# GpSimd masks two more units of softmax weights per step in the first attention layer, and TensorE two fewer

## The chip, the cores and the metric
The kernel runs on one core of a Trainium2 chip. Time is device time in microseconds (us) of one execution; the median of several runs is given. The core has TensorE (PE, matrix products; its weight loads are shown apart as PEld), VectorE (DVE), ScalarE (ACT), GpSimd (POOL) and SyncE (SP), which here only issues DMAs. Each engine works through its own instructions in order, and they wait for each other by semaphores.

## The reference
A Flamingo block of two layers on 32 sequences of 112 tokens with 256 features: cross attention to 375 context rows (16 heads of 16), then a feed-forward part, and the same again with other weights and a mixture of experts. The part that the change touches is the first layer's attention, with one mask of keys for all sequences:

```python
q = split_heads(input_q @ w_q)          # (32, 16, 112, 16)
k = split_heads(input_k @ w_k)          # (32, 16, 375, 16)
v = split_heads(input_v @ w_v)
scores = jnp.einsum('bhqd,bhkd->bhqk', q, k) / jnp.sqrt(jnp.float32(D_K))
scores = jnp.where(mask == 0, jnp.float32(NEG), scores)
attn = jax.nn.softmax(scores, axis=-1)
per_head = jnp.einsum('bhqk,bhkd->bhqd', attn, v)
...
x = x + jnp.tanh(g_xattn[0]) * _L0_xattn_ref(_layernorm(x, axis=-1), ctx_1024, ctx_1024, mask_1x1xSxS2_ik1, ...)
```

A masked key must get the weight zero. That can be done in two ways: add a large negative number to its score ahead of the exponential, or multiply the weight by zero behind it.

## The kernel before, in words
The phases follow each other: weights are prepared, attention of layer 0 (about 85 to 552 us), the first feed-forward part, attention of layer 1, the experts. `attention_phase` is used for both layers.

Attention goes by steps, written out one after the other for each engine (`run_quads`, `body`), 32 sequences and a few steps more. Step s works on several sequences at once, at different stages: the context of sequence s is split into a high and a low half-precision part, the keys of sequence s-1 are made, the values and the row maxima of sequence s-3, the weights of sequence s-4 (d in the code), the output of sequence s-5. So step 4 is the first one that masks weights, and step 35 the last; steps 32 to 35 have no context left to split.

The weights of a sequence are made transposed, with 125 keys on the partitions, in 12 units: unit i is 4 heads (i // 3) by one third of the keys (i % 3), 125 x 448 numbers. For each unit:
- TensorE makes the scores in one of three banks, two products of 224 columns (`score_unit`, L944). If the unit is not in `pool_units`, it first puts the mask there by a product of mask_add with the identity, 448 columns (L940), and the scores are added on top.
- ScalarE takes the exponential into probs (`weigh_up`, L1100).
- If the unit is in `pool_units`, GpSimd multiplies probs in place by mask_keep, 0 or 1 (`mask_unit`, L724).
- At the end of the step TensorE multiplies all 12 units in order with the values (`weigh`, L962), and waits for each unit's mask or exponential as it comes to it. There is only one probs tile: the first exponential of the next step waits until these products are done.

GpSimd's step is: the masks of the units in `pool_units`, in order, and then `low_context`, twice (L789): the low part of the context, that is the input less its high part. TensorE's `make_keys` of the next step waits for both (L850 is its first product), between the first unit and the second:

```python
for i in pool_units:
    ...
    if d.exists(B):
        mask_unit(d, i)
if s.exists(B):
    low_context(s, 0)
    low_context(s, 1)
```

TensorE's step begins with `turn_maxima` of the second half (L923), unit 0, score row 2 and the first keys; score rows (L914) are what VectorE reduces to row maxima (L1272). Twice a step VectorE writes eight maxima negated to max_parts (`shift_parts`, L1281). The keys are copied by ScalarE (`high_keys`, L1108), which then goes on with units 1 to 4. SyncE's step begins with the store of turned maxima (L643) and the load of a context (`load_context`, L649), which waits for the low parts of the sequence that used the buffer before.

In layer 1 the same table of units holds; GpSimd there has the routing to the experts as well.

Of the kernel before, what the change touches and what calls it, by code (L numbers as in the profile page):

```python
# [36 lines left out]
NOBODY = 8192  # L37

POOL_UNITS = (0, 1, 3, 4, 6, 7, 9, 10)
W_SCALE = 2.0 ** 6  # L40
MASKED = float(2 ** 30)
EPS = 1e-5
# [107 lines left out]
def setup_phase(nc, m, a):  # L150


    with ExitStack() as ctx:
# [55 lines left out]
        def _(dve):  # L209
# [35 lines left out]
            for i, ((w, n), tile) in enumerate(raw.items()):  # L245
                dve.wait_ge(high_ready, i + 1)
                dve.scalar_tensor_tensor(out=m["w" + w][n][1][:, :, :], in0=tile[:, :, :], scalar=W_SCALE,
                                         in1=m["w" + w][n][0][:, :, :], op0=ALU.mult, op1=ALU.subtract)
# [7 lines left out]
            for n in range(2):  # L256
                dve.tensor_scalar(m["wo"][n][:, :, :], m["wo"][n][:, :, :], m["gate"][:, n:n + 1], None, ALU.mult)
                scale = 1.0 if n else W_SCALE
                dve.tensor_scalar(bo[n][:, :], bo[n][:, :], m["gate"][0:S, n:n + 1], scale, ALU.mult,
# [10 lines left out]
        def _(act):  # L270
# [4 lines left out]
            for (w, n), tile in raw.items():  # L275
                act.activation(m["w" + w][n][0][:, :, :], tile[:, :, :], ACT.Copy, scale=W_SCALE).then_inc(high_ready, 1)

# [221 lines left out]
def attention_phase(nc, m, layer, x_in, x_out, context, masks, q_split, mask_in, routing):  # L499
# [3 lines left out]
    with ExitStack() as ctx:  # L503
# [82 lines left out]
        work_bank = m["bank"][7]  # L586
        HALF = UNITS // 2
        HH = H // 2
        pool_units = POOL_UNITS

        ctx_rows = context.rearrange("b (c p) k -> b p c k", p=P)
        q_rows = q_split.rearrange("e g (r p) (b t) -> e b (g r) p t", p=NP, t=S)
# [34 lines left out]
        def reduced_at(quad, name):  # L627

            return len(REDUCED) * quad + REDUCED.index(name) + 1
# [86 lines left out]
        def _(pool):  # L716
# [47 lines left out]
            def pick(quad):  # L764
                slots = slice(G * (quad % 3), G * (quad % 3) + G)
                pool.wait_ge(reduced, reduced_at(quad, "inverse"))
                pool.tensor_scalar(sent_rows[:, slots, D], chance[:, :], m["gate"][0:S, 3:4], W_SCALE ** -2,
                                   ALU.mult, ALU.mult).then_inc(combined, 1)
# [302 lines left out]
        def _(act):  # L1071
# [17 lines left out]
            def copy_values(x, e, ks):  # L1089
# [3 lines left out]
                               work_bank[0:CK, 0:D * len(ks)].rearrange("p (k h r) -> p k h r", r=DK, h=H),  # L1093
                               ACT.Copy, scale=1 / W_SCALE).then_inc(v_ready, 1)

# [7 lines left out]
            def high_keys(p, j):  # L1103

                if j == 0:
                    wait(act, k_loaded[p.two], 96 * p.use2)
                act.wait_ge(k_made, KC * p.value + j + 1)
                act.activation(k_high[p.two][:, j, 0:S2], work_bank[:, 0:S2], ACT.Copy,  # L1108
                               scale=1 / W_SCALE).then_inc(k_high_ready, 1)

# [814 lines left out]
```

## Time and profile before
| | |
|---|---|
| Time, median of 3 runs | 1663.68 us (1658.14 to 1667.85) |
| Profiled execution | 1670.54 us, span 1668.9 us |
| TensorE busy | 1486.5 us, 89% of the span |
| VectorE busy | 1067.6 us, 64% |
| GpSimd busy | 853.8 us, 51% |
| ScalarE busy | 818.5 us, 49% |
| Granted TensorE clock, mean | 0.955 of full speed |

Durations of instructions overlap: a product of 448 columns is shown with 0.35 us, and the next one starts 0.19 us after it. So a cost is read from the distance between starts, not from a duration. "Idle before" in a row is the time in which the engine stood still just before it, with the engine and instruction that ended that wait. Layer 0's attention from 200 to 500 us is 22 equal steps.

### The profile page before, as it was taken

To read this page: it belongs to the slowest core of one execution; us is meant where nothing else is said; L and a number is where in the kernel's file an instruction comes from. 1 tells how busy PE (TensorE), PEld (TensorE's weight loads), DVE (VectorE), ACT (ScalarE), POOL (GpSimd) and SP (SyncE) were. 2 spreads that over 40 slices of the span, in tenths; PEclk is the share of its full clock that TensorE was granted. 3 is DMA by queue.
4 is the path that set the end of the run, shared out by engine and by line. 5 is a ranking of instruction groups with operands and counts; after the bars stand their busy time and mean duration, and the time that the engine had idled before them with its cause. 6 is when DMAs were issued, how large, how long until landed. Compare 5 with 4: busy or idle time off the path is not lost. (4 is left out here: it accounts for less than half of the span.)

```text
span 1668.9 us, 41243 instructions
## 1 busy us (share of the span) xinstructions
PE 1486.5 (89%) x15435; PEld 1082.2 (65%) x15435; DVE 1067.6 (64%) x3580; ACT 818.5 (49%) x1907; POOL 853.8 (51%) x904
## 2 busy tenths in 40 slices
PE   0889899999999499999994789999999999529997
PEld 0457678777777266666663457777777777417776
DVE  5767677777777255555545677777777777226663
ACT  3456566666666222222221456666667666314442
POOL 0077677777777000000000177778888888723442
PEclk9999899999999699999997999999999999759999
DMA  5755544544441222222214866655566553063440
GB/s 147 197 130 147 124 102 104 101 102 102 101 93 39 61 63 63 63 71 63 62 36 117 203 125 115 116 113 110 113 128 122 121 108 57 21 187 101 155 137 19
DMA packets 214248, 172.67 MB, mean 103 GB/s; under 512 B 69930, under 2 KB 207599, under 8 KB 214056
## 3 DMA queue, kind: packets, MB, share of 16 engines
q1 hardware_dynamic: 208424, 160.34, 41.8%
q0 software_dynamic: 5632, 9.78, 1.9%
q8 instruction: 119, 1.95, 0.5%
q14 instruction: 73, 0.60, 0.1%
HBM read 95.86 MB, written 41.15 MB: 82 GB/s over the span
## 5 line engine op out<-in xcount | busy, mean ns | idle before, releaser
L1100 ACT ACTIVATE probs_a<-bank 125x448 f32<-125x448 f32 x768 | 384.7, 540 | 23.7 <-PE bank L944 15.0
L724 POOL TENSOR_TENSOR probs_a<-probs_a,mask_keep 125x448 int32<-125x448 int32 x256 | 285.5, 1138 | 108.2 <-ACT probs_a L1100 108.1
L1272 DVE CUSTOM_DVE_ANT_0 masked_scores_a<-bank,mask_add_a 112x375 bf16<-112x375 f32 x512 | 262.5, 547 | 106.0 <-PE bank L914 105.5
L724 POOL TENSOR_TENSOR probs_a<-probs_a,keep_a 125x448 int32<-125x448 int32 x256 | 286.1, 1137 | 66.4 <-ACT probs_a L1100 65.0
L1272 DVE CUSTOM_DVE_ANT_0 masked_scores_a<-bank,mask_add 112x375 bf16<-112x375 f32 x512 | 261.1, 550 | 85.5 <-PE bank L914 82.0
L914 PE MATMUL bank<-k_stack_a,q_stack_a 96*128 96x375 f16 x1024 | 292.4, 326 | 5.8 <-DVE row_max_a L1272 4.6
L944 PE MATMUL bank<-q_stack_a,k_stack_a 97*128 97x224 f16 x1536 | 254.6, 261 | 11.7 <-DMA q_stack_a<-max_t_a 10.7
L944 PEld LDWEIGHTS bank<-q_stack_a,k_stack_a 97*128 97x128 f16 x1536 | 147.0, 99 | 72.7 <-DMA q_stack_a<-max_t_a 12.3
L789 POOL TENSOR_TENSOR ctx_low_a<-ctx_in_a,ctx_high_a 128x375 f16<-128x375 f32 x128 | 113.1, 904 | 146.2 <-ACT ctx_high_a L1078 146.1
L1627 PE MATMUL bank<-h0h_f,ffn_w 128*128 128x448 f16 x512 | 180.5, 352 | 0.0
L1627 PE MATMUL bank<-h0l_f,ffn_w 128*128 128x448 f16 x512 | 180.4, 352 | 0.0
L1466 POOL DMA_DIRECT2D x_after_ffn<-y_f x8 | 5.9, 741 | 333.7 <-DVE y_f L1513 333.7
L962 PE MATMUL bank<-probs_a,values_a 125*32 125x112 f32 x6144 | 161.5, 260 | 1.9 <-POOL probs_a L724 1.9
L962 PEld LDWEIGHTS bank<-probs_a,values_a 125*32 125x32 f32 x6144 | 144.8, 110 | 22.6 <-issue 19.5
L1153 ACT ACTIVATE heads_t_a<-bank 128x448 f32<-128x448 f32 x64 | 34.8, 544 | 216.7 <-PE bank L962 216.7
L914 PEld LDWEIGHTS bank<-k_stack_a,q_stack_a 96*128 96x128 f16 x1024 | 99.5, 98 | 45.2 <-DVE row_max_a L1272 13.7
L1578 ACT ACTIVATE h1h_f<-bank 128x448 f16<-128x448 f32 x64 | 34.8, 544 | 152.9 <-PE bank L1627 152.9
L871 PE MATMUL bank<-wv_high,ctx_high_a 128*128 128x256 f16 x384 | 105.3, 274 | 1.4 <-DVE k_low_a L1315 1.4
L871 PE MATMUL bank<-wv_high,ctx_low_a 128*128 128x256 f16 x384 | 104.9, 273 | 0.0
L871 PE MATMUL bank<-wv_low,ctx_high_a 128*128 128x256 f16 x384 | 104.7, 273 | 0.0
L1506 DVE SCALAR_TENSOR_TENSOR h1l_f<-bank,h1h_f 128x448 f16<-128x448 f32 x64 | 39.8, 621 | 97.3 <-ACT h1h_f L1578 97.3
L850 PE MATMUL bank<-ctx_high_a,wk_high 128*128 128x375 f16 x256 | 84.2, 329 | 6.9 <-DVE k_low_a L1315 6.6
(215 smaller groups left out, 3193.0 us busy)
## 6 DMA issues: line engine op xcount, KB each, us to landing
k_stack_a<-k_high_a SPq DMA_DIRECT2D x256, 96.0 KB, 4.0
ctx_in_a<-in_ctx_dram SPq DMA_DIRECT2D x64, 375.0 KB, 3.6
w_in_e<-in_L_ffn_W_dram SPq DMA_DIRECT2D x16, 1024.0 KB, 8.6
k_stack_a<-k_low_a SPq DMA_DIRECT2D x128, 96.0 KB, 4.5
q_stack_a<-q_split SPq DMA_DIRECT2D x128, 84.0 KB, 3.4
q_split<-high_a SPq DMA_DIRECT2D x32, 224.0 KB, 3.7
mask_in_f<-in_mask_BxSxS_if_dram SPq DMA_DIRECT2D x8, 656.2 KB, 6.4
mask_keep<-keep_f SPq DMA_DIRECT2D x8, 656.2 KB
```

Of the source, the lines that this page charges most:

```text
L724: pool.tensor_tensor(bits, bits, cols, ALU.mult).then_inc(masked, 1)
L789: pool.tensor_tensor(ctx_low[s.four][:, cols], ctx_in[s.two][:, c, :], ctx_high[s.four][:, cols], ALU.subtract).then_inc(ctx_low_ready, 1)
L850: last = pe.matmul(work_bank[:, 0:S2], w[:, c, j * P:(j + 1) * P], part[p.four][:, c * S2:(c + 1) * S2], start=c == 0 and n == 0, stop=c = ...
L871: last = pe.matmul(work_bank[:, (k % 2) * D:(k % 2 + 1) * D], part[x.four][:, at:at + P], w[:, c, :], start=c == 0 and n == 0, stop=c == K ...
L914: pe.matmul(bank_of(x, h)[:, 0:S2], q_stack[x.four][0:STACK, at:at + P], k_stack[x.four][0:STACK, (h // 2) * WIDE:(h // 2) * WIDE + S2], s ...
L944: last = pe.matmul(bank[:, half * 2 * S:(half + 1) * 2 * S], k_stack[d.four][0:ROWS, at:at + P], q_stack[d.four][0:ROWS, (2 * t + half) * ...
L962: last = pe.matmul(head_bank[QUAD * j:QUAD * (j + 1), t * S:(t + 1) * S], values[d.two][:, k, 4 * t + j, :], probs[:, i, j * S:(j + 1) * S ...
L1100: act.activation(probs[:, i, :], score_bank[i % 3][0:CK, 0:GT], ACT.Exp, scale=DK ** -0.5).then_inc(exped, 1)
L1153: act.activation(heads_t[:, :], head_bank[:, 0:GT], ACT.Copy).then_inc(heads_ready, 1)
L1272: dve.tensor_tensor_reduce(masked_scores[:, use_of[x.value, h] % 3, :], bank_of(x, h)[0:S, 0:S2], mask_add[x.four][:, 0:S2], 1.0, -LARGEST ...
L1506: dve.scalar_tensor_tensor(out=low[:, j, :], in0=z_bank[z % 4][:, 0:GT], scalar=0.0, in1=high[:, j, :], op0=ALU.max, op1=ALU.subtract).the ...
L1627: last = pe.matmul(z_bank[z % 4][:, 0:GT], w[layer][:, c, j * P:(j + 1) * P], part[:, c, :], start=c == 0 and n == 0, stop=c == chunks - 1 ...
```

## The change
Layer 0 gets a table of its own, with units 2 and 5 in it as well. Layer 1 keeps the old one.

```diff
 POOL_UNITS = (0, 1, 3, 4, 6, 7, 9, 10)
+POOL_UNITS_0 = (0, 1, 2, 3, 4, 5, 6, 7, 9, 10)
...
-        pool_units = POOL_UNITS
+        pool_units = POOL_UNITS if layer else POOL_UNITS_0
```

All later lines of the code move down by one, so L724 of before is L725 of after.

On GpSimd, in layer 0 at the last two steps with low parts and behind them; L724 is a mask, L789 a low part. Before:

```order
L724 TENSOR_TENSOR probs_a<-probs_a,mask_keep 125x448 x8
L789 TENSOR_TENSOR ctx_low_a<-ctx_in_a,ctx_high_a 128x375 x2
L724 TENSOR_TENSOR probs_a<-probs_a,mask_keep 125x448 x8
L789 TENSOR_TENSOR ctx_low_a<-ctx_in_a,ctx_high_a 128x375 x2
L724 TENSOR_TENSOR probs_a<-probs_a,mask_keep 125x448 x32
L1381 UNCONDITIONAL_BRANCH
```

And after:

```order
L725 TENSOR_TENSOR probs_a<-probs_a,mask_keep 125x448 x10
L790 TENSOR_TENSOR ctx_low_a<-ctx_in_a,ctx_high_a 128x375 x2
L725 TENSOR_TENSOR probs_a<-probs_a,mask_keep 125x448 x10
L790 TENSOR_TENSOR ctx_low_a<-ctx_in_a,ctx_high_a 128x375 x2
L725 TENSOR_TENSOR probs_a<-probs_a,mask_keep 125x448 x40
L1382 UNCONDITIONAL_BRANCH
```

Two more masks stand ahead of each pair of low parts, and the four steps without low parts have 40 masks in place of 32.

On TensorE, in a middle step of layer 0, right behind the first keys: L914 is a score row, L944 the scores of a unit, L940 a mask added by a product. Here units 1, 2, 3 and 4 are scored. Before:

```order
L914 MATMUL bank<-k_stack_a,q_stack_a 128x375
L944 MATMUL bank<-q_stack_a,k_stack_a 128x224 x2
L914 MATMUL bank<-k_stack_a,q_stack_a 128x375
L940 MATMUL bank<-ident_b,mask_add 128x448
L944 MATMUL bank<-q_stack_a,k_stack_a 128x224 x4
L914 MATMUL bank<-k_stack_a,q_stack_a 128x375 x2
L944 MATMUL bank<-q_stack_a,k_stack_a 128x224 x2
```

And after:

```order
L915 MATMUL bank<-k_stack_a,q_stack_a 128x375
L945 MATMUL bank<-q_stack_a,k_stack_a 128x224 x2
L915 MATMUL bank<-k_stack_a,q_stack_a 128x375
L945 MATMUL bank<-q_stack_a,k_stack_a 128x224 x4
L915 MATMUL bank<-k_stack_a,q_stack_a 128x375 x2
L945 MATMUL bank<-q_stack_a,k_stack_a 128x224 x2
```

The mask's product ahead of unit 2 is gone. Later in the same step, at unit 5, ahead of the turning of the heads (L970). Before:

```order
L914 MATMUL bank<-k_stack_a,q_stack_a 128x375 x2
L940 MATMUL bank<-ident_b,mask_add 128x448
L944 MATMUL bank<-q_stack_a,k_stack_a 128x224 x2
L914 MATMUL bank<-k_stack_a,q_stack_a 128x375
L970 MATMUL bank<-ident,heads_t_a 112x128 x4
```

And after:

```order
L915 MATMUL bank<-k_stack_a,q_stack_a 128x375 x2
L945 MATMUL bank<-q_stack_a,k_stack_a 128x224 x2
L915 MATMUL bank<-k_stack_a,q_stack_a 128x375
L971 MATMUL bank<-ident,heads_t_a 112x128 x4
L945 MATMUL bank<-q_stack_a,k_stack_a 128x224 x4
```

Here the one ahead of unit 5 is gone. The products for units 8 and 11 stay.

## Rows read from the trace of the kernel before

**Rows 1.** Table of windows: one middle step, and a step near the end of layer 0.

```profile
core 0: us, PE busy (x) PEld busy (x) DVE busy (x) ACT busy (x) POOL busy (x), PEclk, DMA share, GB/s
200.00:213.63 13.63, 13.63 (x187) 10.88 (x185) 10.33 (x41) 9.04 (x23) 10.66 (x11) 1.00 0.49 104
512.00:524.00 12.00, 11.52 (x170) 9.10 (x169) 9.96 (x38) 6.82 (x17) 8.83 (x8) 1.00 0.08 21
```

**Rows 2.** Timeline, GpSimd, one step: start, duration, instruction, count, [idle before, releaser].

```profile
321.42 1.13 POOL L724 TENSOR_TENSOR probs_a<-probs_a,mask_keep 125x448 int32<-125x448 int32 x1 [2.07 <-ACT probs_a L1100]
322.74 3.33 POOL L724 TENSOR_TENSOR probs_a<-probs_a,mask_keep 125x448 int32<-125x448 int32 x3 [0.18 <-ACT probs_a L1100]
326.38 3.33 POOL L724 TENSOR_TENSOR probs_a<-probs_a,mask_keep 125x448 int32<-125x448 int32 x3 [0.31 <-ACT probs_a L1100]
330.12 1.13 POOL L724 TENSOR_TENSOR probs_a<-probs_a,mask_keep 125x448 int32<-125x448 int32 x1 [0.41 <-ACT probs_a L1100]
331.21 1.76 POOL L789 TENSOR_TENSOR ctx_low_a<-ctx_in_a,ctx_high_a 128x375 f16<-128x375 f32 x2
335.05 1.13 POOL L724 TENSOR_TENSOR probs_a<-probs_a,mask_keep 125x448 int32<-125x448 int32 x1 [2.08 <-ACT probs_a L1100]
```

**Rows 3.** Timeline, TensorE, the same step.

```profile
320.52 0.32 PE L850 MATMUL bank<-ctx_high_a,wk_high 128*128 128x375 f16 x1
...
322.00 0.35 PE L940 MATMUL bank<-ident_b,mask_add 112*128 112x448 bf16 x1
322.19 0.55 PE L944 MATMUL bank<-q_stack_a,k_stack_a 97*128 97x224 f16 x4
...
331.30 2.51 PE L962 MATMUL bank<-probs_a,values_a 125*32 125x112 f32 x96
...
334.15 0.32 PE L850 MATMUL bank<-ctx_high_a,wk_high 128*128 128x375 f16 x1
```

**Rows 4.** Timeline, all engines, the start of step 4.

```profile
102.45 1.75 POOL L789 TENSOR_TENSOR ctx_low_a<-ctx_in_a,ctx_high_a 128x375 f16<-128x375 f32 x2
...
104.25 0.10 PEld L850 LDWEIGHTS bank<-ctx_high_a,wk_high 128*128 128x128 f16 x1 [0.32 <-POOL ctx_low_a L789]
104.28 0.52 PE L850 MATMUL bank<-ctx_high_a,wk_high 128*128 128x375 f16 x1
```

**Rows 5.** Timeline, ScalarE, behind the key start of 334.15.

```profile
335.37 0.49 ACT L1108 ACTIVATE k_high_a<-bank 128x375 f16<-128x375 f32 x1 [0.40 <-PE bank L850]
335.75 1.88 ACT L1100 ACTIVATE probs_a<-bank 125x448 f32<-125x448 f32 x4
```

**Rows 6.** Timeline, GpSimd, steps 33, 34 and 35.

```profile
512.33 8.89 POOL L724 TENSOR_TENSOR probs_a<-probs_a,mask_keep 125x448 int32<-125x448 int32 x8 [3.79 <-ACT probs_a L1100]
525.01 8.89 POOL L724 TENSOR_TENSOR probs_a<-probs_a,mask_keep 125x448 int32<-125x448 int32 x8 [3.80 <-ACT probs_a L1100]
537.35 8.80 POOL L724 TENSOR_TENSOR probs_a<-probs_a,mask_keep 125x448 int32<-125x448 int32 x8 [3.45 <-ACT probs_a L1100]
```

**Rows 7.** Timeline, TensorE, the products with the values of the same steps.

```profile
521.26 2.51 PE L962 MATMUL bank<-probs_a,values_a 125*32 125x112 f32 x96
...
533.60 2.51 PE L962 MATMUL bank<-probs_a,values_a 125*32 125x112 f32 x96
...
546.20 0.59 PE L962 MATMUL bank<-probs_a,values_a 125*32 125x112 f32 x16 [0.69 <-POOL probs_a L724]
```

**Rows 8.** Timeline, VectorE's max_parts in a middle step and near the end, and TensorE.

```profile
339.82 0.16 DVE L1281 TENSOR_SCALAR max_parts_a<-row_max_a 112x8 f16<-112x8 f32 x1
...
515.64 1.13 DVE L1281 TENSOR_SCALAR max_parts_a<-row_max_a 112x8 f16<-112x8 f32 x1
...
528.32 1.14 DVE L1281 TENSOR_SCALAR max_parts_a<-row_max_a 112x8 f16<-112x8 f32 x1
...
517.29 0.33 PE L914 MATMUL bank<-k_stack_a,q_stack_a 96*128 96x375 f16 x1 [0.34 <-DVE row_max_a L1272]
```

**Rows 9.** Timeline, TensorE, the wait in step 8.

```profile
172.89 0.93 PE L944 MATMUL bank<-q_stack_a,k_stack_a 97*128 97x224 f16 x4 [7.24 <-DMA q_stack_a<-max_t_a]
```

**Rows 10.** Timeline, SyncE, behind the key start of 334.15.

```profile
334.57 0.69 SPq L643 DMA_DIRECT2D q_stack_a<-max_t_a  x1
335.63 0.40 SPq L649 DMA_DIRECT2D ctx_in_a<-in_ctx_dram  x1
```

## The prediction, on record before the run
> **What bounds the kernel now.** I read the table of windows first, then GpSimd's timeline over one step of layer 0, then TensorE's over the same step, and last the end of the layer. The reader is to see four things.
>
> First, in the middle of layer 0 TensorE is busy for all of a step's 13.63 us at a granted clock of 1.00, and GpSimd for 10.66 us [rows 1]. TensorE is the bound there, and what it no longer does shortens the step, as long as nobody is later than it.
>
> Second, GpSimd's 10.66 us are eight masks and two low parts of the context, with four gaps: 2.07, 0.18, 0.31 and 0.41 us [rows 2]. One step later the same row stands at 335.05 in place of 321.42, which gives the 13.63 us again. Masks that follow each other start 1.095 us apart, (3.33 - 1.14) / 2; the two low parts take 1.76 us together.
>
> Third, the low parts are not free to be late. TensorE's first key product of the next step waits for both of them (ctx_low_ready in make_keys), and so does SyncE's next load of the context, which stands behind another DMA at 335.63 anyway [rows 10]. Now they end at 331.21 + 1.76 = 332.97 and that product starts at 334.15 [rows 2, 3]: 1.18 us of slack. I call the start of that first product the key start; it is at 320.52 and 334.15.
>
> Fourth, in the last three steps there are no low parts and no keys, GpSimd's masks run without a gap, and in the very last step the products with the values wait for them [rows 6, 7].
>
> **The change, part by part.** *Removed on TensorE:* two products with the identity per step, for units 2 and 5. One costs the distance to the next product, 322.19 - 322.00 = 0.19 us [rows 3]; so 0.38 us a step, and TensorE alone would need 13.25 us. The two are at 322.00 and in the same place ahead of unit 5; both lie between the key start and the products with the values.
>
> *Added on GpSimd:* two masks, 2 x 1.095 = 2.19 us a step. The gaps take some of it. Before mask 0 the gap stays, since that weight can't be made before the old step's products with the values have released the buffer. The gap before mask 1 stays too. After it eight further masks stand in place of six, and the gaps of 0.31 and 0.41 us close. Are the exponentials there in time? ScalarE makes units 1 to 4 in 1.88 us from 335.75 [rows 5], so they keep ahead of masks 1.095 us apart. Unit 10's used to be there at 330.12, 9.60 us after the key start, and its mask now comes up at 2.22 + 8 x 1.095 = 10.98 us. So masks 1 to 10 run without a gap.
>
> *The loop that this closes.* Mask 1 is tied to the key start: keys, then ScalarE's copy of them at 335.37, then unit 1's exponential in ScalarE's order [rows 5], then mask 1, 322.74 - 320.52 = 2.22 us after the key start [rows 2, 3]. From there: nine masks, 9 x 1.095 = 9.86 us; two low parts, 1.76 us; and the wake of TensorE. That wait has one occurrence in the trace before: the low parts end at 102.45 + 1.75 = 104.20 and the waiting product starts at 104.28 [rows 4], 0.08 us. Together 2.22 + 9.86 + 1.76 + 0.08 = 13.92 us from one key start to the next. This is above TensorE's 13.25 and above the 13.63 of today: the step gets longer, by 0.29 us, though TensorE has less to do.
>
> *VectorE's small instruction.* max_parts (L1281) takes 0.16 us where GpSimd is in a gap (339.82), but 1.13 and 1.14 us where it is issued within a row of masks (515.64, 528.32) [rows 8]. Its end then falls on a mask's end: 525.01 + 4 x 1.095 + 0.04 = 529.43, and 528.32 + 1.14 = 529.46. GpSimd pays as well: its eight masks take 8.89 us with one such meeting and 8.80 us without [rows 6], 0.09 us each. A step has two of them, and with no gaps left both will meet a mask: the loop becomes 13.92 + 2 x 0.085 = 14.09 us, 0.46 us over today. I take this value. For VectorE the first of the two is issued about 5.4 us after the key start (339.82 - 334.15 = 5.67, less 0.19 to 0.38 for the earlier products), and the next mask starts at 2.22 + 3 x 1.095 = 5.51. Just ahead of it the wait is 0.1 us, just behind it a whole mask. In the second case the row maxima come 1 us late; TensorE has 13.25 us of work in a loop of 14.09, so 0.84 us of that hides.
>
> The Trainium skill, page "SBUF — State Buffer", section "Who interferes with whom", says that VectorE and GpSimd share one pair of ports as an exclusive lock, held for a whole instruction, and that the loser blocks fully rather than slows. The rows above agree, with 1.14 us for 0.16. Without this rule the sum would be the 13.92 us alone.
>
> *Are the products with the values held up?* They start at 331.30, 10.78 us after the key start, now 10.40. They take 2.51 us for twelve units [rows 3], so unit 10 comes up at about 10.40 + 2.0 = 12.4 us. Its mask ends at 10.98 + 1.14 + 0.17 = 12.29. No wait, by 0.1 us; were there one, it would lie within the 0.84 us.
>
> *The clock.* In 512 to 524 us TensorE was busy for 11.52 of 12.00 us and the granted clock stayed at 1.00 [rows 1]; I take nothing for it. The other bound is what stood behind the wait of 7.24 us in step 8: four score products took 0.93 us in place of 0.55 [rows 3, 9], a drop that lasted some us; behind waits nine times shorter I expect none.
>
> *How often.* Steps 4 to 31 have masks and low parts, so their low parts hold 28 key starts (of steps 5 to 32), with 27 distances between them. One of those, in step 8, holds a DMA wait of 7.2 us on TensorE [rows 9], which dissolves the loop: the time lost there before the key start, 0.84 us, is had back. Sum: 26 x 0.46 = +12.0; step 8, -0.8; the first step, whose GpSimd still had larger gaps, about -0.3 of the TensorE saving; step 32, which has no low parts, -0.4.
>
> *The last three steps.* Step 33: masks start at 512.33, ten take 9 x 1.1 + 1.14 + 0.09 and end at 523.5. Unit 10 used to come up at 521.26 + 2.0 = 523.3; so 0.2 us later. Step 34: from 525.01 the end is 536.1, unit 10 was up at 533.60 + 2.0 = 535.6: 0.5 us. Step 35: TensorE already waits for mask 10 (546.20) [rows 6, 7]: the full 2.2 us. Together +2.9.
>
> Total: 12.0 - 0.8 - 0.3 - 0.4 + 2.9 = +13.4 us. Against the profiled execution, 1670.5 us (span 1668.9), that is 1683.9. This execution lies 6.8 us above the median shown, 1663.7; I add the same 13.4 to the median, and the forecast is 1663.7 + 13.4 = 1677 us. A measurement of this kernel tells 0.5%, about 8.3 us, from no change.
>
> **The rivals.**
> - *Port meetings cost GpSimd nothing.* The loop is 13.92 us: 26 x 0.29 = 7.5, less 0.7, 0.3 and 0.4, plus 2.9, is +9 us, 1673. For it: one difference of 0.09 us is thin evidence. Against: it stands in two steps alike.
> - *VectorE decides.* Both max_parts wait for a whole mask (1.14 us) on the path of the score rows; TensorE's step is 13.25 + 1.1 = 14.35 us, 0.72 over today. 26 x 0.72 = 18.7, plus 1.5 for the ends, is +20 us, 1684. For it: in the last steps TensorE waited for a row maximum right behind such a meeting (517.29 [rows 8]). Against: the second one comes late in the step, where 0.7 us remain. It would rest on the same rule of the Trainium skill, page "SBUF — State Buffer".
> - *No change.* Mask 1 comes less than 2.22 us after the key start once TensorE has waited, or the low parts' wake costs less, so that the loop ends near 13.63: only the tail pays, +3 us, 1667. Against: three engines in series stand in these 2.22 us.
> - *Faster.* GpSimd fits, and the step takes TensorE's 13.25 us: 28 x -0.38 = -10.6, plus 2.9, is -8 us, 1656. It needs the loop below 13.25, that is 0.84 us gone from it: the low parts would have to stand earlier, or masks to start 0.09 us closer than the 1.095 that every group of three shows. For it: GpSimd's sum of work, 10 x 1.095 + 1.76 = 12.7 us, is below 13.25, and someone who looks at busy time alone finds that it fits. Against: mask 1 can't start before 2.22 us, so only a part of the step is open to it. It decides from the key start's wait: none at L850, and it has won.
>
> **How the numbers follow.** Forecast (1677) 0.45; VectorE decides (1684) 0.20; free port meetings (1673) 0.15; no change (1667) 0.13; faster (1656) 0.07. The range 1666 to 1686 takes in all but the faster case and a little on each side. Slower by over 0.5% (above 1672): 0.45 + 0.20 + 0.09 = 0.74, since the 1673 case lies at the border. Within 0.5%: 0.19. Faster: 0.07. The forecast's own range is 1672 to 1682.
>
> **What would show it.** In the profile after: key starts 14.1 us apart (13.9 without the port's share, 14.35 with VectorE in charge); a wait of some 0.8 us per step of the first key product (L850) for GpSimd's ctx_low_a, on an engine that had none; ten masks as one and nine with a gap of about 1.2 us between; max_parts at 0.2 to 1.1 us in place of 0.16 to 0.22; step 35's masks 11 us long. TensorE's waits for ctx_low_a near zero would make me wrong, as would gaps in masks 1 to 10 that I haven't foreseen, or a granted clock under 1.00 between 200 and 500 us.

## The result, and the profile after

The changed kernel takes 1680.2 us (median of 6 runs, 1678.4 to 1682.1); the kernel before, run beside it, takes 1664.7 (6 runs, 1658.1 to 1667.9). The ratio is 1.0091, with a 95% interval of 1.0074 to 1.0108: slower by 12 to 18 us. The forecast was 1677 and the range 1666 to 1686. The profiled execution of the changed kernel took 1681.3 us, its span 1679.6.

In the changed kernel all lines stand one number higher: the masks are L725, the low parts L790, the key products L851.

I read the table of windows over the middle of layer 0 first. Its columns are those of [rows 1]; this is the kernel after.

```profile
200.00:500.00 300.00, 290.77 (x3984) 224.82 (x3984) 230.15 (x866) 190.82 (x473) 275.42 (x260) 1.00 0.49 100
```

Before, TensorE was busy for the whole of a step [rows 1]. Now it lacks 9.2 of 300 us, at the same granted clock of 1.00, and GpSimd is busy for 92% of the time in place of 78% (10.66 of 13.63). No engine is full, which means that a chain over several engines sets the step. The table of waits of the same stretch names the link that was not there before. Its columns: engine, what it writes, its line, what it waited for; us in total, times, longest.

```profile
ACT heads_t_a L1154 <- PE bank L963: 69.0, 21, 3.3
DVE masked_scores_a L1273 <- PE bank L915: 59.5, 64, 1.4
POOL probs_a L725 <- ACT probs_a L1101: 24.6, 42, 1.1
ACT k_high_a L1109 <- PE bank L851: 20.9, 21, 1.3
PEld bank L851 <- POOL ctx_low_a L790: 15.0, 20, 0.8
...
PE bank L851 <- POOL ctx_low_a L790: 8.7, 20, 0.4
```

The fifth line is TensorE's weight load ahead of the first key product, waiting for the low parts of the context 20 times, 0.75 us each. The larger waits above it are those of engines that wait for TensorE's or ScalarE's work of the same step.

GpSimd's timeline over one step, kernel after, answers to [rows 2] (start, duration, instruction, count, [idle before, releaser]):

```profile
334.42 1.13 POOL L725 TENSOR_TENSOR probs_a<-probs_a,mask_keep 125x448 int32<-125x448 int32 x1 [0.35 <-ACT probs_a L1101]
336.36 9.89 POOL L725 TENSOR_TENSOR probs_a<-probs_a,mask_keep 125x448 int32<-125x448 int32 x9 [0.80 <-ACT probs_a L1101]
346.21 1.75 POOL L790 TENSOR_TENSOR ctx_low_a<-ctx_in_a,ctx_high_a 128x375 f16<-128x375 f32 x2
348.33 1.13 POOL L725 TENSOR_TENSOR probs_a<-probs_a,mask_keep 125x448 int32<-125x448 int32 x1 [0.37 <-ACT probs_a L1101]
```

And TensorE's, which answers to [rows 3]:

```profile
334.13 0.33 PE L851 MATMUL bank<-ctx_high_a,wk_high 128*128 128x375 f16 x1 [0.44 <-POOL ctx_low_a L790]
...
348.02 0.33 PE L851 MATMUL bank<-ctx_high_a,wk_high 128*128 128x375 f16 x1 [0.42 <-POOL ctx_low_a L790]
```

The loop can be read off these rows. Key start at 334.13. Mask 1 starts at 336.36, 2.23 us later. The low parts start at 346.21, 9.85 us later, and end at 346.21 + 1.75 = 347.96. The next key start is 0.06 us behind that, at 348.02. A step is 13.89 us, 0.27 more than the 13.62 of before.

VectorE's max_parts in the same step (kernel after), the row that answers to [rows 8]:

```profile
339.48 0.23 DVE L1282 TENSOR_SCALAR max_parts_a<-row_max_a 112x8 f16<-112x8 f32 x1
```

It still takes 0.23 us, not 1.13, though masks now stand in a row there. It was issued 5.35 us after the key start. The next mask starts at 336.36 + 3 x 1.095 = 339.65 and the one running ends 0.04 us behind that, at 339.69 (masks overlap a little in the rows), and max_parts ends at 339.71: it waited for the end of a mask, and that end came soon.

The last three steps, GpSimd after, against [rows 6]:

```profile
515.41 10.98 POOL L725 TENSOR_TENSOR probs_a<-probs_a,mask_keep 125x448 int32<-125x448 int32 x10 [2.08 <-ACT probs_a L1101]
528.28 10.99 POOL L725 TENSOR_TENSOR probs_a<-probs_a,mask_keep 125x448 int32<-125x448 int32 x10 [1.89 <-ACT probs_a L1101]
541.16 10.96 POOL L725 TENSOR_TENSOR probs_a<-probs_a,mask_keep 125x448 int32<-125x448 int32 x10 [1.89 <-ACT probs_a L1101]
```

and TensorE after, against [rows 7]:

```profile
526.45 0.59 PE L963 MATMUL bank<-probs_a,values_a 125*32 125x112 f32 x16 [0.58 <-POOL probs_a L725]
...
539.32 0.59 PE L963 MATMUL bank<-probs_a,values_a 125*32 125x112 f32 x16 [0.69 <-POOL probs_a L725]
...
552.17 0.97 PE L963 MATMUL bank<-probs_a,values_a 125*32 125x112 f32 x16 [0.49 <-POOL probs_a L725]
553.81 1.10 PE L971 MATMUL bank<-ident,heads_t_a 128*112 128x128 f32 x4 [0.66 <-ACT heads_t_a L1154]
```

Now the products with the values wait for a mask in all three steps. The last row also shows something that the prediction had not counted. The four transposes behind the last products take 1.10 us. Before, they took:

```profile
547.46 0.65 PE L970 MATMUL bank<-ident,heads_t_a 128*112 128x128 f32 x4 [0.67 <-ACT heads_t_a L1153]
```

The windows over this end give the granted clock, the third number from the end: first the kernel before, then the kernel after.

```profile
546.00:552.00 6.00, 3.39 (x29) 2.28 (x29) 1.09 (x4) 0.90 (x2) 0.15 (x1) 0.82 0.00 0
```

```profile
552.00:559.00 7.00, 4.45 (x29) 2.88 (x29) 1.07 (x3) 0.90 (x2) 0.12 (x1) 0.50 0.00 0
```

After the change TensorE runs its last 29 instructions of the layer at the lower level (0.50, that is 1.2 GHz). The other two traces of each kernel agree: from the end of the last products with the values to the layer's last output the granted clock is 0.77, 0.69 and 0.70 before, and 0.50 three times after.

**Where the time went, by segments.** Each kernel was profiled three times, once here and twice in the experiments (e7 and e12 are the kernel before, e4 and e11 the changed one). A segment is cut at key starts and at the end of x_sum, layer 0's last output (551.98 + 0.42 before, 559.00 + 0.42 after). Means of three, us:

| segment | before | after | difference |
|---|---|---|---|
| start to the key start of step 5 | 117.9 | 117.1 | -0.7 (spread before 116.9 to 119.8) |
| step 5 to step 9 | 63.8 | 64.8 | +0.9 |
| step 9 to step 32, 23 steps | 313.8 | 320.1 | +6.4 |
| step 32 to layer 0's last output | 54.7 | 58.2 | +3.6 |
| to layer 1's first key start | 362.8 | 363.9 | +1.1 |
| layer 1 to its last output | 525.6 | 528.2 | +2.5 (before 523.1 to 527.0, after 525.5 to 530.0) |
| rest | 226.3 | 225.2 | -1.1 |
| span | 1664.8 | 1677.5 | +12.6 |

The steps of layer 0 that the prediction spoke of take 11 us more (432.2 to 443.1, no overlap in three traces each). The runs say 12 to 18. What lies between is in layer 1 and in the ends, where executions of one and the same kernel differ by 4 us.

### The profile page after: what moved, and what is told of

Same layout as the page of the kernel before. It is cut to its first block and busy times, and to the rows that moved or that the text cites. A ratio compares the mean times of both kernels' runs of the same rounds, so it can differ in the third digit from the quotient of the medians.

```text
span 1679.6 us, 41179 instructions
## 1 busy us (share of the span) xinstructions
PE 1475.4 (88%) x15371; PEld 1063.7 (63%) x15371; DVE 1067.9 (64%) x3580; ACT 813.3 (48%) x1907; POOL 919.4 (55%) x968
## 5 line engine op out<-in xcount | busy, mean ns | idle before, releaser
L725 POOL TENSOR_TENSOR probs_a<-probs_a,mask_keep 125x448 int32<-125x448 int32 x320 | 353.0, 1138 | 49.6 <-ACT probs_a L1101 49.6
L725 POOL TENSOR_TENSOR probs_a<-probs_a,keep_a 125x448 int32<-125x448 int32 x256 | 285.9, 1135 | 70.8 <-ACT probs_a L1101 69.3
L945 PE MATMUL bank<-q_stack_a,k_stack_a 97*128 97x224 f16 x1536 | 253.7, 260 | 16.8 <-DMA q_stack_a<-max_t_a 15.5
L790 POOL TENSOR_TENSOR ctx_low_a<-ctx_in_a,ctx_high_a 128x375 f16<-128x375 f32 x128 | 112.8, 903 | 143.6 <-ACT ctx_high_a L1079 143.6
L851 PE MATMUL bank<-ctx_high_a,wk_high 128*128 128x375 f16 x256 | 84.3, 329 | 18.6 <-POOL ctx_low_a L790 11.5
```

Of the source, the lines that this page charges most:

```text
L725: pool.tensor_tensor(bits, bits, cols, ALU.mult).then_inc(masked, 1)
L790: pool.tensor_tensor(ctx_low[s.four][:, cols], ctx_in[s.two][:, c, :], ctx_high[s.four][:, cols], ALU.subtract).then_inc(ctx_low_ready, 1)
L851: last = pe.matmul(work_bank[:, 0:S2], w[:, c, j * P:(j + 1) * P], part[p.four][:, c * S2:(c + 1) * S2], start=c == 0 and n == 0, stop=c = ...
L945: last = pe.matmul(bank[:, half * 2 * S:(half + 1) * 2 * S], k_stack[d.four][0:ROWS, at:at + P], q_stack[d.four][0:ROWS, (2 * t + half) * ...
```

## The experiments

Each kernel's rows have the line numbers of its own code. "Step" is the distance between two key starts in the middle of layer 0, "steps 5 to 35" is the time from the key start of step 5 to the layer's last output: 432.0 to 432.6 us in three traces of the kernel before, 442.9 to 443.4 in three of the changed one. The kernel before took 1667.5 us on the chip of e1 to e4, 1665.1 on that of e7 to e10 and 1665.9 on that of e5, e6, e11 and e12 (17, 23 and 19 runs). A ratio is that to the kernel before on the same chip.

**e1_nine_units.** One unit goes back to TensorE.

```
-POOL_UNITS_0 = (0, 1, 2, 3, 4, 5, 6, 7, 9, 10)
+POOL_UNITS_0 = (0, 1, 2, 3, 4, 6, 7, 9, 10)
```

> Only unit 2 moves to GpSimd (nine masks a step in layer 0), unit 5 stays with TensorE. Low-parts theory (the step is as long as the loop key start, exponential of unit 1, masks, two low parts, next key start; measured 13.90 us with ten masks): with nine masks the loop is 13.90 - 1.10 = 12.80 us, below TensorE's 13.63 - 0.19 = 13.44. So TensorE bounds again, no wait of the first key product for ctx_low_a, key starts 13.44 us apart: 28 x -0.19 = -5.3, plus 1.1 us in step 35 where the masks end last, is -4 us against before (ratio 0.997 to 0.998). Port theory (each max_parts that meets a mask costs the step, since there are fewer gaps): key starts 13.6 us or more apart, ratio 1.000 or above. GpSimd-late-for-the-values theory: a wait of the products with the values for a mask in middle steps.

Measured: 1679.3 us, ratio 1.0069 (1.0051 to 1.0087), a step of 14.00 us: longer than with ten units. The expectation fell. There is no wait for the low parts. What TensorE waits for is in the table of waits between 200 and 500 us:

```profile
PEld bank L915 <- DVE row_max_a L1273: 12.8, 22, 0.6
```

and VectorE's and TensorE's timelines of one step show why:

```profile
314.92 1.13 DVE L1282 TENSOR_SCALAR max_parts_a<-row_max_a 112x8 f16<-112x8 f32 x1
```

```profile
316.56 0.10 PEld L915 LDWEIGHTS bank<-k_stack_a,q_stack_a 96*128 96x128 f16 x1 [0.59 <-DVE row_max_a L1273]
```

The key start is at 309.39, so max_parts is issued 5.53 us after it, 0.18 us later than in the changed kernel: one product with the identity now stands ahead (0.19 us [rows 3]). The next mask starts at 311.60 + 3 x 1.095 = 314.89, so max_parts missed that moment by 0.03 us and waited for the whole mask. The row maxima behind it on VectorE came late, and TensorE lost 0.6 us a step. 13.44 + 0.6 is 14.0. This is my rival "VectorE decides", not for the changed kernel but for its neighbour.

GpSimd's eight masks behind mask 0 take 0.09 us more than the least that eight need (8.80 us [rows 6]):

```profile
311.60 8.89 POOL L725 TENSOR_TENSOR probs_a<-probs_a,mask_keep 125x448 int32<-125x448 int32 x8 [0.19 <-ACT probs_a L1101]
```

This is not a price of the meeting. The first seven start 1.09 us apart, those behind the meeting too. Only the last, of unit 10, starts 1.19 us behind the one before it, and 0.08 us behind the end of its own exponential (318.74 + 0.54 = 319.28 on ScalarE, the mask at 319.35). It waited for ScalarE.

**e2_low_parts_before_9.** The low parts are made ahead of units 9 and 10.

```
 for i in pool_units:
+    if i == 9 and not layer and s.exists(B):
+        low_context(s, 0)
+        low_context(s, 1)
...
-if s.exists(B):
+if s.exists(B) and layer:
     low_context(s, 0)
```

> Ten masks as in the change, but in layer 0 GpSimd makes the two low parts ahead of units 9 and 10 in place of behind them. GpSimd's work per step is the same. If GpSimd's work alone set the step (10 masks and two low parts are 12.7 us, plus start-up gaps), it would stay at 13.9 us. By the theory that the last wait counts: the first key product no longer waits, but the products with the values wait for mask 10, and behind them come unit 0, the keys (0.41 us), unit 1's exponential (2.22 us), seven masks, two low parts and two masks: 0.5 + 0.41 + 2.22 + 8 x 1.097 + 1.76 + 1.14 = 14.8 us per step. That is 26 x 1.17 = 30 us over before, plus 2.9 in the last steps: +33 us, ratio 1.02.

Measured: 1705.5 us, ratio 1.0232 (1.0208 to 1.0257), a step of 14.82 us. GpSimd's and TensorE's timelines:

```profile
307.77 7.72 POOL L725 TENSOR_TENSOR probs_a<-probs_a,mask_keep 125x448 int32<-125x448 int32 x7 [0.19 <-ACT probs_a L1104]
315.43 1.78 POOL L790 TENSOR_TENSOR ctx_low_a<-ctx_in_a,ctx_high_a 128x375 f16<-128x375 f32 x2
317.14 2.24 POOL L725 TENSOR_TENSOR probs_a<-probs_a,mask_keep 125x448 int32<-125x448 int32 x2
```

```profile
304.61 0.59 PE L966 MATMUL bank<-probs_a,values_a 125*32 125x112 f32 x16 [0.69 <-POOL probs_a L725]
...
319.44 0.59 PE L966 MATMUL bank<-probs_a,values_a 125*32 125x112 f32 x16 [0.69 <-POOL probs_a L725]
```

What was late changes places: the low parts are in time, unit 10's mask ends at 317.14 + 2.24 = 319.38, and the last products with the values start 0.06 us behind it. GpSimd does the same 12.7 us of work in either order. So it is the order in which the work ends, against who waits for it, that sets the step.

**e3_low_parts_first.** Ten masks as in the changed kernel, and in layer 0 the low parts ahead of them: ScalarE splits the context at the start of its step, and GpSimd makes the low parts first, in a time in which it waited for the old step's products with the values.

```
+if s.exists(B) and not layer:
+    low_context(s, 0)
+    low_context(s, 1)
 for i in pool_units:
...
-if s.exists(B):
+if s.exists(B) and layer:
     low_context(s, 0)
...
+if s.exists(B) and not layer:
+    split_context(s, 0)
+    split_context(s, 1)
 if e.exists(B):
```

> Ten masks as in the change. In layer 0 ScalarE splits the next context at the start of its step (where it waits for the products with the values) and GpSimd makes the low parts ahead of mask 0 (where it waits for unit 0's exponential), so the low parts are ready almost a step ahead of the keys that need them. Low-parts theory: the wait at the first key product goes, the masks of a step end 2.22 + 8 x 1.097 + 1.14 = 12.13 us after its key start and unit 10 comes up at 12.43, so TensorE bounds with 13.25 us per step: 28 x -0.375 = -10.5, plus 2.9 in the last steps, is -8 us against before, ratio 0.995. If GpSimd's total of busy time and unavoidable gaps is the bound, or VectorE behind the port: key starts stay 13.6 to 14.1 us apart, ratio 1.000 to 1.01.

Measured: a step of 13.29 us, the 13.25 that TensorE alone needs, and no wait for the low parts. GpSimd:

```profile
302.50 1.13 POOL L725 TENSOR_TENSOR probs_a<-probs_a,mask_keep 125x448 int32<-125x448 int32 x1 [0.34 <-ACT probs_a L1104]
303.82 9.91 POOL L725 TENSOR_TENSOR probs_a<-probs_a,mask_keep 125x448 int32<-125x448 int32 x9 [0.19 <-ACT probs_a L1104]
313.69 1.75 POOL L790 TENSOR_TENSOR ctx_low_a<-ctx_in_a,ctx_high_a 128x375 f16<-128x375 f32 x2
315.80 1.14 POOL L725 TENSOR_TENSOR probs_a<-probs_a,mask_keep 125x448 int32<-125x448 int32 x1 [0.35 <-ACT probs_a L1104]
```

The low parts at 313.69 are those of the step that begins here; they have a whole step until they are wanted. The mechanism holds: ten masks fit when the low parts are out of the loop. The time was expected at 0.995 and is 1667.1 us, ratio 1.0005 (0.9990 to 1.0019). The trace gives 427.3 us for steps 5 to 35, 5 less than before; there 23 steps give back 7.3 (306.5 in place of 313.8) and the last ones take 2.9 more (57.5). The five us do not show in the median of the runs. Where they are lost I can't say: the other segments of its one trace lie within the spread of the others, and the execution traced was the fastest of the twelve (1662.0 us, of 1662.0 to 1672.2), so no trace shows a middle one.

**e4_change_again.** The changed kernel unaltered, on the chip of e1 to e3.

> The changed kernel once more, unchanged. The two profiles of before and after differ by 10.7 us, the medians of the runs by 15.5. If what is beyond the 8 to 10 us that layer 0's steps explain is noise of the start and of layer 1, then key starts are 13.90 us apart here too, and the part from the first key start of step 5 to the end of layer 0's attention is 443 us as in the first profile, while the start and layer 1 differ by some us. If it belongs to the change, layer 1 takes 3 us more here as well.

Measured: 1680.7 us, ratio 1.0079 (1.0057 to 1.0102), a step of 13.91 us, steps 5 to 35 in 443.1, and layer 1 in 529.0.

**e5_low_first_eight.** The order of e3 with the eight masks of before.

```
-pool_units = POOL_UNITS if layer else POOL_UNITS_0
+pool_units = POOL_UNITS
```

> The order of the run with the low parts first (ScalarE splits the context at the start of its step, GpSimd makes the low parts ahead of mask 0), but with the eight masks of the kernel before. Low-parts theory: in the kernel before nobody waited for the low parts, so the order by itself gives nothing: key starts 13.63 us apart, from the key start of step 5 to layer 0's last output 432 us, ratio 1.000. If the order itself had made the gain (ScalarE relieved in the middle of its step), key starts are below 13.5 us here too.

Measured: 1667.1 us, ratio 1.0013 (0.9997 to 1.0028), a step of 13.62 us, steps 5 to 35 in 433.7. The order alone gives nothing while TensorE is full. The 0.33 us between e5 and e3 is thus what the two masks take off TensorE, for 0.38 in the forecast. Of the three orders tried with whole low parts, only this one has it.

**e6_half_low_part.** The changed kernel with a shorter second low part, one column in place of 375, from step 4 of layer 0 on.

```
-cols = slice(c * S2, (c + 1) * S2)
-pool.tensor_tensor(ctx_low[s.four][:, cols], ctx_in[s.two][:, c, :], ...
+n = 1 if c == 1 and s.value >= 4 and not layer else S2
+cols = slice(c * S2, c * S2 + n)
+pool.tensor_tensor(ctx_low[s.four][:, cols], ctx_in[s.two][:, c, 0:n], ...
```

> The changed kernel with ten masks and its own order, but from step 4 on GpSimd computes of the second low part one column in place of 375 (the other columns keep what they held), 0.8 us less at the end of its step. No other engine's work or order changes. Low-parts theory: the loop of 13.90 us falls to 13.1, below TensorE's own; the first key product no longer waits for ctx_low_a, and key starts are 13.29 us apart as in the run with the low parts first: from the key start of step 5 to layer 0's last output 443 - 16 = 427 us, ratio to before 0.997 to 1.000. If the wait for ctx_low_a only took the place of another wait of the same length, key starts stay near 13.9 us, ratio 1.008.

Measured: 1663.8 us, ratio 0.9988 (0.9974 to 1.0002), a step of 13.29 us, steps 5 to 35 in 427.7. GpSimd:

```profile
316.24 9.89 POOL L725 TENSOR_TENSOR probs_a<-probs_a,mask_keep 125x448 int32<-125x448 int32 x9 [0.19 <-ACT probs_a L1103]
326.10 1.04 POOL L792 TENSOR_TENSOR ctx_low_a<-ctx_in_a,ctx_high_a 128x375 f16<-128x375 f32 x2
```

The low parts take 1.04 us in place of 1.75. The loop would be 13.90 - 0.71 = 13.19 us, and TensorE's own 13.29 takes over. A cut of 0.71 us in GpSimd's chain takes 0.61 us off the step, which shows the chain through the low parts to be the bound of the changed kernel.

**e7_before_again.** The kernel before, unaltered.

> The kernel before, unchanged, for a second profile of it. Its first profile lay 6.8 us above the median then shown, the profiles of the changed kernel near theirs. If layer 0's steps explain the change, key starts in layer 0 are 13.63 us apart again and the rest of the program (before the first key start of step 5, and from layer 0's last output on) differs by some us from one execution to the next, with no sign that follows the change. Ratio 1.000.

Measured: 1666.6 us, layer 1 in 523.1, ratio to itself 1.0016 (1.0004 to 1.0028). An interval here can miss 1 by a small amount, so I take no difference under 0.3% for real.

**e8_nine_units_reduce.** e1 with max_parts made by another instruction, a reduction over one element with the sign changed, in layer 0.

```
-dve.tensor_scalar(max_parts[:, half, 0:HH], row_max[:, cols], -1.0, None, ALU.mult)...
+dve.tensor_reduce(max_parts[:, half, 0:HH], row_max[:, cols].unsqueeze(2), AX.X, ALU.max,
+                  negate=True)...
```

> Nine masks a step (unit 2 moved, unit 5 not), and in layer 0 VectorE writes max_parts with a reduction over one element, negated, in place of the product with -1: the same numbers by another form of instruction. With nine masks alone, key starts were 14.00 us apart, max_parts took 1.13 us and TensorE waited 0.6 us a step for a row maximum. Port theory (the product with -1 waits for GpSimd's running mask, and the row maxima behind it come late): the reduction takes some 0.1 us within masks too, that wait of TensorE goes, and key starts are 13.44 us apart, 28 x -0.19 + 1.1 = -4 us against before, ratio 0.997. If the 1.13 us are something else (VectorE waits for max_turned, or for its own row maxima), nothing changes: 14.00 us, ratio 1.007.

Measured: 1663.4 us, ratio 0.9991 (0.9982 to 1.0001), a step of 13.48 us in place of 14.00 (expected: 0.997 and 13.44). One row of VectorE, one of GpSimd:

```profile
310.71 0.15 DVE L1285 TENSOR_REDUCE max_parts_a<-row_max_a 112x8 f16<-112x8 f32 x1
```

```profile
320.88 8.80 POOL L725 TENSOR_TENSOR probs_a<-probs_a,mask_keep 125x448 int32<-125x448 int32 x8 [0.18 <-ACT probs_a L1101]
```

max_parts takes 0.15 us in the middle of the masks, and the wait for the row maxima is gone. The masks take 8.80 in place of 8.89, since unit 10's exponential is now there in time. Between e1 and e8 lies the form of one VectorE instruction, and 13 us by the two ratios: steps 5 to 35 take 430.5 in place of 445.1. The Trainium skill, page "SBUF — State Buffer", section "Who interferes with whom", says that a tensor_reduce never contends with GpSimd on this chip while a tensor_scalar can; this pair of runs agrees, with 0.15 against 1.13 us.

**e9_low_first_short_tail.** e3, with the reduction of e8, and fewer masks on GpSimd in the last three steps: eight in steps 33 and 34, four in step 35. The counts that TensorE waits for are summed to fit.

```
+POOL_UNITS_LAST = (0, 2, 4, 6)
...
+def units_of(value):
+    if layer or value < B - 3:
+        return pool_units
+    return POOL_UNITS if value < B - 1 else POOL_UNITS_LAST
```

> The version that the runs so far point to: ten masks a step with the low parts made ahead of mask 0 (key starts 13.29 us apart in the run before), max_parts as a reduction, and fewer masks in the last three steps, where GpSimd ends last: eight in steps 33 and 34, four (units 0, 2, 4, 6) in step 35. Steps: 26 x -0.34 = -8.8 us. Last steps: step 35 ends with ScalarE's exponentials and not with the masks, -2 us in place of +2.9. Together -11 us against before, ratio 0.993. If the time between other phases swallows it as in the run with the low parts first (ratio 1.0005 where its steps gave -5 us in the trace), ratio 0.996 or more.

Measured: 1653.5 us (6 runs), ratio 0.9926 (0.9910 to 0.9942). It beats both kernels. Which of its three parts gives how much was not tried one by one; e3 has the same step without the reduction. The step is 13.29 us, steps 5 to 35 take 420.9, and of these step 32 to the end 50.8 in place of 54.7 before. TensorE is busy for all of the middle, and GpSimd too for 95%:

```profile
200.00:500.00 300.00, 299.79 (x4118) 237.12 (x4120) 236.67 (x905) 206.97 (x493) 286.11 (x270) 1.00 0.49 104
```

In the last step the masks are done after 4.43 us, and the products with the values run without a wait for them:

```profile
526.84 4.43 POOL L736 TENSOR_TENSOR probs_a<-probs_a,mask_keep 125x448 int32<-125x448 int32 x4 [3.02 <-ACT probs_a L1115]
```

```profile
531.94 2.51 PE L977 MATMUL bank<-probs_a,values_a 125*32 125x112 f32 x96
```

**e10_max_parts_later.** The changed kernel with a short VectorE instruction, of no use to the result, ahead of the first max_parts of a step.

```
+dve.tensor_reduce(spare[:, :], mask_add[0][:, 0:192], AX.X, ALU.max)
 shift_parts(x, 0)
```

> The changed kernel, with one small reduction more on VectorE ahead of the first max_parts of a step in layer 0 (0.2 to 0.3 us; its result is not used). In the changed kernel that max_parts is issued 5.35 us after the key start, 0.16 us ahead of the next mask's start at 5.51, and takes 0.23 us. Port theory: now it is issued behind 5.51 and waits for the whole mask, about 1 us; the row maxima come 1.1 us late, TensorE waits for one of them, and the step becomes 13.29 + 0.8 = 14.1 us with little of a wait for ctx_low_a left: +0.2 us a step, +5 us over the changed kernel, ratio to before 1.011. If VectorE has slack and its instruction's place doesn't matter: 13.90 us and the changed kernel's ratio, 1.008 to 1.009.

Measured: 1688.4 us, ratio 1.0153 (1.0135 to 1.0172), a step of mostly 14.37 us. VectorE:

```profile
316.50 0.34 DVE L1354 TENSOR_REDUCE spare_a<-mask_add 112x1 f32<-112x192 bf16 x1
316.76 1.06 DVE L1283 TENSOR_SCALAR max_parts_a<-row_max_a 112x8 f16<-112x8 f32 x1
...
323.79 1.23 DVE L1283 TENSOR_SCALAR max_parts_a<-row_max_a 112x8 f16<-112x8 f32 x1
```

The waits between 200 and 500 us, and GpSimd's masks of that step with its low parts behind them:

```profile
PEld bank L916 <- DVE row_max_a L1274: 16.2, 21, 0.8
PEld bank L925 <- DVE max_parts_a L1283: 8.0, 16, 0.5
```

```profile
313.37 9.90 POOL L726 TENSOR_TENSOR probs_a<-probs_a,mask_keep 125x448 int32<-125x448 int32 x9 [0.43 <-ACT probs_a L1102]
323.22 1.77 POOL L791 TENSOR_TENSOR ctx_low_a<-ctx_in_a,ctx_high_a 128x375 f16<-128x375 f32 x2
```

The key start is at 311.16, so max_parts is issued at 5.60 us, 0.25 later than in the changed kernel, 0.1 us behind the start of a mask at 5.50. It waits for that mask, as expected. The expected step was 0.3 us too short, because the second max_parts of the step, moved by the first, now waits too: issued at 323.79, during the first of the two low parts, it ends at 325.02, just behind the second (323.22 + 1.77 = 324.99). TensorE waits for it in turn, 16 times in 21 steps. So the changed kernel stays clear of the long wait by less than 0.25 us; its rows say 0.16, and e1's say that 0.18 is too much.

The nine masks of this step take 9.90 us though VectorE waited for a whole one of them; they took 9.89 where it had not. GpSimd pays nothing for a meeting.

**e11_change_third** and **e12_before_third.** A third trace of each kernel, one run each.

> The changed kernel, a third profile, for the spread of layer 1: 530.0 and 529.0 us from its first key start to its last output in the two profiles so far, against 527.0 and 523.1 of the kernel before. If layer 1 is only noise, this one can lie anywhere from 520 to 530; if it follows the change, it is at 529 again.

> The kernel before, a third profile, for the spread of layer 1: if layer 1 is only noise, its length can be anywhere from 520 to 530 us; if it follows the change, 523 to 527. Layer 0 from the key start of step 5 to its last output: 432 us again.

Measured: 1676.3 us with steps 5 to 35 in 442.9, and 1666.3 us with 432.0. These are the third members of the table above. Layer 1 took 525.5 us in the changed kernel's trace and 526.8 in the other, so the 530 and 529 of the two earlier traces of the changed kernel do not come every time. Most of it is noise; a difference of some 2 us in the mean can't be excluded.

## Why the prediction was right, and where its steps were off

The forecast was +13.4 us; the medians differ by 15.5 us (12 to 18), the spans of three traces each by 12.6. Right in sign, size and mechanism. But that the size came out so near is in part luck: a term of 4.4 us was wrong, and it was made up by a clock that was not counted, a gain in step 8 that did not come, and some us outside the steps of layer 0. Without that term the sum would have been +9 us, as in the first rival. Step by step:

- **The loop, 13.92 us.** Its parts came out at 2.23 + 9.85 + 1.75 + 0.06 = 13.89 us for 2.22 + 9.86 + 1.76 + 0.08. Each had been read from one row of the kernel before, the wake of TensorE from a single occurrence in step 4. e6 shows that this loop is the bound, and e3 that it is the place of the low parts which closes it.
- **Port meetings, 2 x 0.085 us: the mis-sized term.** It was to make the step 14.09 us. Both max_parts do meet a mask in every step (0.23 and 0.21 us), but GpSimd pays nothing: nine masks take 9.89 us, and 8 x 1.095 + 1.13 is 9.89. e10 shows that a wait for a whole mask costs GpSimd nothing either (9.90). The 0.09 us that I had read from 8.89 against 8.80 [rows 6] was something else. In step 33 VectorE meets the mask that runs at 515.64, while the extra time stands ahead of the last mask, at 520.08. That mask starts 0.08 us behind the end of its own exponential, 519.47 + 0.54 = 520.01 (kernel before, ScalarE and GpSimd):

```profile
519.47 0.54 ACT L1100 ACTIVATE probs_a<-bank 125x448 f32<-125x448 f32 x1
520.08 1.13 POOL L724 TENSOR_TENSOR probs_a<-probs_a,mask_keep 125x448 int32<-125x448 int32 x1
```

  The row of eight masks hides this wait, since it is shown as one piece; so "without a gap" was not right for steps 33 and 34. The agreement of two steps was no evidence for a price, as both have the same order of work. The loop that ran is that of my first rival. Term: +12.0 forecast for 26 distances, about 26 x 0.27 = +7.0 by the measured step.
- **Step 8, -0.8: not seen.** Steps 5 to 9 take 0.9 us more, near what four longer steps give (1.1) without a gift. In this trace TensorE waited for 7.42 us there in place of 7.24:

```profile
169.83 0.93 PE L945 MATMUL bank<-q_stack_a,k_stack_a 97*128 97x224 f16 x4 [7.42 <-DMA q_stack_a<-max_t_a]
```

  In the other two traces of the changed kernel (e4, e11) it waited for 6.95 and 7.00 us, and in those of the kernel before (e7, e12) for 7.25 and 7.28. So a part of the gift may be there, but step 8 as a whole is no shorter: 23.40, 22.82 and 22.96 us in place of 23.41, 22.65 and 22.73. What the DMA's moment depends on was not tried.
- **The first step, -0.3.** Start to step 5 varies by 3 us between traces of the kernel before; it can't be told.
- **Steps 33 and 34, +0.2 and +0.5.** Here the sign and size were right. The distances of the products with the values, taken at the end of all of them, grew from 12.68 to 12.87 us and from 12.34 to 12.88: +0.19 and +0.54.
- **Step 35, +2.2.** Its masks take 10.96 in place of 8.80 us: +2.16.
- **The clock, taken as nothing: about +1.0 us missed.** I had looked at the wait of step 8 and at 512 to 524 us, but not at what comes behind the last, longer wait for masks. From the last mask's end to the layer's last output it was 6.25 us before (546.15 to 552.40) and is 7.31 after (552.12 to 559.43), with the granted clock at 0.50 in place of 0.82 and the same 29 instructions; the means of three traces are 6.34 and 7.32 us. With the 0.3 us saved in step 32 (0.4 forecast) the end is 3.6 us longer, for 2.5 forecast.
- **Sum.** From step 5 to the end of layer 0 +11.0 us, for +13.7 forecast (13.4 and the first step's 0.3): 26 x 0.17 = 4.4 less for the port, 0.8 more for step 8, 1.0 more for the clock, which makes 11.1. The runs' 15.5 us is reached only with some us outside these steps. Layer 1 took between 519.9 and 530.0 us in the fourteen traces, though its code was the same in all of them; whether the changed kernel costs 2 us there or none stays open.
- **The signs.** Key starts 13.9 apart as named for the case without the port's share; the wait for the low parts 0.75 us for 0.8; step 35's masks 11 us as said. The gap between mask 0 and the nine was 0.80 us, not 1.2, and the gap before mask 0, which was to stay at 2.07 us, shrank to 0.35; the loop runs through neither. "The granted clock under 1.00 between 200 and 500 us" did not come.
- **The rival "faster"** named its own condition, that the low parts would have to stand earlier. e3 and e9 fulfil it, and the step falls to 13.29 us. The spacing of the masks stayed at (9.91 - 1.14) / 8 = 1.096 us.
- **The rival "VectorE decides"** was given 0.20. It did not happen, by 0.16 us, and happened in e1 and e10; e10's step of 14.37 us is near the 14.35 of this rival, though there the second wait is one for the low parts. A change of one unit (e1) that should have been a compromise was as slow as the change itself, through another wait.

## What to carry to other kernels

Before work goes to an engine with a lower busy share, draw the loop that runs through it from one step to the next, and add the new work to that: GpSimd had 3 us free per step and took 2.2 more, and the step grew by 0.27 us, because its last work of a step was waited for. Put what is wanted next step into the engine's own waits first (e3), and lessen its share again in the last steps, where nothing hides it (e9); the two, with e8's form of max_parts, turned a loss of 0.9% into a gain of 0.7%. And where a very short VectorE instruction stands among GpSimd's, compare its moment of issue with the starts of the other's instructions, or take a form that does not meet them (e8). Before a small difference between two merged rows becomes a price, find out where in the row it stands: the 0.09 us here stood four masks behind the meeting that I gave it to.

## What the runs showed of the hardware

- A tensor_scalar of 112x8 on VectorE takes 0.16 us alone, 0.23 when issued 0.16 us ahead of the start of GpSimd's next mask, and 1.13 when issued 0.03 us behind one (e1). In 400 meetings with a mask in the traces here, issued 0.14 us or more ahead of GpSimd's next start, it was let in at the end of the running mask even though GpSimd's next instruction was already waiting. Of 25 that were issued less than 0.1 us ahead of the next mask, ten waited for the whole of it.
- That rule is not the same behind a low part: in e10, issued 0.26 to 0.30 us ahead of the second low part, it waited for both in 21 steps and was let in between them in the others.
- GpSimd lost nothing by such meetings: nine masks took 9.89 us where VectorE had come just ahead of an end and 9.90 where it had waited for a whole mask (e10).
- The same values made by a tensor_reduce over one element took 0.15 us in the midst of masks (e8). With nine masks the step was 14.00 us with the one form and 13.48 with the other.
- TensorE's granted clock behind the last products with the values went with the waits for masks within them. With 1.2 us of waits in all (four traces, the kernel before and e5) it was 0.69 to 0.78 from their end to the layer's last output; with 1.9 us (e3) 0.59; with 2.1 us or more (eight traces, the changed kernel's among them) 0.50 or 0.51; without a wait (e9) 0.91. Between the kernel before and the changed one this cost 1.0 us.
